# A residual attention block with a three-cycle coupling network: the later weights' loads move behind the first transposes of x, and every engine's list of steps is in a new order

## What is computed

```python
def reference(x, ctx, ...):
    x = x + xattn(layernorm(x), ctx, ctx, Wq, bq, Wk, bk, Wv, bv, Wo, bo, phase)
    return x + ffn(layernorm(x), cn_w1, ..., gc_b3, adaptive_range)

def xattn(q, k, v, ...):
    qh, kh, vh = heads(q @ Wq.T + bq), heads(k @ Wk.T + bk), heads(v @ Wv.T + bv)
    qh, kh = phase_sync(qh, phase), phase_sync(kh, phase)
    attn = softmax(einsum('bhqd,bhkd->bhqk', qh, kh) / sqrt(32))
    return merge(einsum('bhqk,bhkd->bhqd', attn, vh)) @ Wo.T + bo

def ffn(x, ...):
    gf = global_net(x.mean(axis=1))            # gelu, gelu, sigmoid
    out = x
    for _ in range(3):
        tf = coupling_net(out)                 # w1, w2, w3 with gelu, w4 with sigmoid
        coupling = 0.1 + adaptive_range * (0.7 * gf + 0.3 * tf - 0.5) * 2.0
        out = out + coupling * twist(out)      # swaps quarters of the columns
    return out
```

## Time and profile before

| | us |
|---|---|
| median of 3 runs | 1389.52 |
| lowest, highest | 1389.43, 1393.32 |
| the profiled execution | 1389.49 |
| its span, first to last instruction | 1387.7 |
| PE busy (of the span) | 1248.0 (90%) |
| DVE busy | 1071.4 (77%) |
| ACT busy | 1059.0 (76%) |
| POOL busy | 624.0 (45%) |

### The profile page before, as it was taken

The page is one execution under the profiler, slowest core; times in us unless marked ns, Lnnn a source line. Parts: engine busy times, 40 slices in busy tenths (PEclk is TensorE's granted clock), DMA queues, the critical chain, the costliest instruction groups (busy, mean ns, idle before and its releaser), DMA issues.

```text
span 1387.7 us, 27846 instructions
## 1 busy us (share of the span) xinstructions
PE 1248.0 (90%) x10392; PEld 863.4 (62%) x10392; DVE 1071.4 (77%) x2125; ACT 1059.0 (76%) x1912; POOL 624.0 (45%) x491
## 2 busy tenths in 40 slices
PE   7776889989999899999999899999999899999984
PEld 5332556657666676658666666657666666657763
DVE  3897449986799769996799769995799759984465
...
DMA packets 319065, 116.54 MB, mean 84 GB/s; under 512 B 301777, under 2 KB 303569, under 8 KB 316882
## 3 DMA queue, kind: packets, MB, share of 16 engines
...
...
## 4 chain that ended last, share of the span: by engine, by line
PE 44%; DVE 18%; ACT 15%; issue 9%; SPq 6%; DMA 6%; POOL 2%; ACTq 0%; DVEq 0%; POOLq 0%
PE ps L369 15%; PE ps L384 9%; PE ps L269 7%; PE ps L318 6%; SPq L3070 3%; PE ps L396 3%; ACT spent L776 2%; DVE xr L1829 2%; DMA x2T<-xr 2%; SPq L3024 2%; PE ps L287 2%; PE ps L404 2%; ACT xr L764 2%; ACT z L848 2%; DVE pr L1871 2%
## 5 line engine op out<-in xcount | busy, mean ns | idle before, releaser
L2869 POOL TENSOR_TENSOR h<-z,h 128x512 f16<-128x512 f32 x192 | 251.3, 1314 | 355.8 <-DVE h L1919 355.8
L369 PE MATMUL ps<-x2T,W 128*128 128x256 f16 x3072 | 350.5, 274 | 5.6 <-ACT Y L835 2.2
L369 PEld LDWEIGHTS ps<-x2T,W 128*128 128x128 f16 x3072 | 297.7, 98 | 54.7 <-issue 9.6
L384 PE MATMUL ps<-h,W 128*128 128x256 f16 x2304 | 275.1, 275 | 12.6 <-POOL h L2869 11.3
L384 PEld LDWEIGHTS ps<-h,W 128*128 128x128 f16 x2304 | 223.5, 99 | 62.7 <-issue 26.5
L2862 POOL TENSOR_TENSOR prob<-prob,rc 128x512 f32<-128x512 f32 x128 | 147.5, 1174 | 140.0 <-DVE rc L1865 140.0
L269 PE MATMUL ps<-xoT,WQ 128*128 128x512 f16 x768 | 176.2, 383 | 16.3 <-DMA xoT<-xr 10.4
L318 PE MATMUL ps<-WO,xoT 128*128 128x512 f16 x768 | 179.6, 384 | 7.2 <-DVE xoT L1876 7.2
L1829 DVE TENSOR_TENSOR xr<-ps,xr 128x512 f16<-128x512 f32 x128 | 87.9, 687 | 82.9 <-ACT xr L764 81.6
L269 PEld LDWEIGHTS ps<-xoT,WQ 128*128 128x128 f16 x768 | 73.6, 98 | 104.6 <-DMA xoT<-xr 11.5
L318 PEld LDWEIGHTS ps<-WO,xoT 128*128 128x128 f16 x768 | 75.0, 99 | 97.7 <-DVE xoT L1876 8.1
...
## 6 DMA issues: line engine op xcount, KB each, us to landing
xin<-x SPq DMA_DIRECT2D x16, 1024.0 KB, 5.2
...
pT<-pr SPq DMA_TRANSPOSE x128, 3.2
wq_s<-wq SPq DMA_DIRECT2D x1, 1024.0 KB, 5.7
wk_s<-wk SPq DMA_DIRECT2D x1, 1024.0 KB, 10.1
```

The lines of the kernel that those rows point to most:

```text
L369: mm = e.matmul(ps[:, BANK_F + L, at * LBLK:(at + 1) * LBLK], w, v, start=(n == 0), stop=(n == 3 * C - 1))
L384: mm = e.matmul(ps[:, BANK_F + L, m * LBLK:(m + 1) * LBLK], w, v, start=(c + m + a == 0), stop=(c == C - 1 and m == C2 - 1 and a == 2))
L2869: e.tensor_tensor(h1[:, L, LO, pair(n)], z[:, L, pair(n)], h1[:, L, HI, pair(n)], ALU.subtract).then_inc(lg[L]["lo1"], 1)
```

## The change

SP gets a new step, `load_late(n)`. The seventeen loads that stood in a row ahead of the first `x_turn` (the output weight and bias, the last rows of weights, three scalars, w1, w2, g1, w3, g2 and five bias columns) are dealt out to five calls of it, behind the first turns of x:

```diff
             load_x(1)
-            load("wo", wo_s[:], by_chunk(woT))
-            load("bo", bo_s[:], row(bo).partition_broadcast(P))
...
-            load("cols", gb2_col[:], gb2)
-            x_turn(0, 0, 0, 0); x_turn(0, 0, 0, 1); x_turn(0, 0, 0, 3); x_turn(0, 0, 0, 2)
-            kv_load(0)
-            kv_store(0, 1)
-            x_turn(0, 0, 1, 0); x_turn(0, 0, 1, 1); x_turn(0, 0, 1, 2); x_turn(0, 0, 1, 3)
+            x_turn(0, 0, 0, 0); x_turn(0, 0, 0, 1); x_turn(0, 0, 0, 2); x_turn(0, 0, 0, 3)
+            load_late(0, 1); load_late(0, 3); load_late(0, 0); load_late(0, 2)
+            x_turn(0, 0, 1, 0)
+            kv_store(0, 1)
+            kv_load(0)
+            x_turn(0, 0, 1, 1)
+            load_late(0, 4)
+            x_turn(0, 0, 1, 3); x_turn(0, 0, 1, 2)
```

All engines' lists are in a new order beyond that. On PE `q(0,0,3)` stands one `vmul` earlier, the first `y` of the network are (0,0,1,0), (0,0,1,1), (0,0,0,0), and in batch 1 `y(0,0,1,3)` goes ahead of `s(1,0)` and an `l2` between `s(1,0)` and `s(1,1)`. On DVE `zero_v` is spread between the first `xl`, `bias_out` is earlier, and the output bias and the last rows of weights come behind `k_lo`. On SP in batch 0:

```diff
-            p_turn(0, 4, 0); p_turn(0, 4, 1); p_turn(0, 5, 0); p_turn(0, 5, 1); p_turn(0, 6, 0); p_turn(0, 6, 1)
-            load_next(0, 0)
-            p_turn(0, 7, 0); p_turn(0, 7, 1)
+            p_turn(0, 4, 0); p_turn(0, 4, 1); p_turn(0, 5, 0); p_turn(0, 5, 1)
+            kv_store(0, 5)
+            p_turn(0, 6, 0)
+            load_next(0, 0)
+            p_turn(0, 7, 0); p_turn(0, 6, 1); p_turn(0, 7, 1)
```

More of the change, by code:

```diff
@@ L1120, in scalar_program @@
             gg(1, 0)
+            t_out(0, 0, 1, 0)
+            act1(1, 0, 0, 0, 0)
+            t_out(0, 0, 1, 1)
+            act1(1, 0, 1, 0, 0)
             act3(0, 1, 1, 2)
-            t_out(0, 0, 1, 0); t_out(0, 0, 1, 1)
             yc(1, 0, 0, 1)
-            act1(1, 0, 0, 0, 0); act1(1, 0, 0, 0, 1); act1(1, 0, 1, 0, 0)
+            act1(1, 0, 0, 0, 1)
+            xn1(2, 0, 0)
             gg(1, 1)
-            t_out(0, 1, 0, 0)
+            xh(2, 0, 0, 0)
             u_(0, 1, 1, 2)
+            cc(0, 1, 1, 2)
@@ L1142, in scalar_program @@
             xh(2, 0, 0, 3)
[L1143 to L1144 removed]
+            yc(1, 0, 0, 3)
+            act1(1, 0, 0, 0, 3)
+            t_out(0, 1, 0, 1)
+            act1(1, 1, 0, 0, 0)
             yc(1, 1, 0, 1)
[L1146 to L1149 removed]
+            act2(1, 0, 0, 0, 0); act2(1, 0, 0, 0, 1)
             xn1(2, 1, 0)
             xh(2, 0, 1, 0)
+            t_out(0, 1, 1, 0)
@@ L1280, in scalar_program @@
                 gg(p, 0)
-                t_out(o, 0, 1, 0); t_out(o, 0, 1, 1)
+                act1(p, 0, 0, 0, 0); act1(p, 0, 1, 0, 0)
+                t_out(o, 0, 1, 0)
+                act3(o, 1, 1, 2)
+                t_out(o, 0, 1, 1)
                 yc(p, 0, 0, 1)
-                act1(p, 0, 0, 0, 0)
-                act3(o, 1, 1, 2)
-                act1(p, 0, 0, 0, 1); act1(p, 0, 1, 0, 0)
+                act1(p, 0, 0, 0, 1)
+                xn1(b, 0, 0)
                 gg(p, 1)
+                xh(b, 0, 0, 0)
@@ L2288, in vector_program @@
-            stats(2, 0, 1, 3)
-            aggr(2, 0, 1, 2); aggr(2, 0, 1, 3)
-            var(2, 0, 1)
-            hi1(1, 0, 0, 0, 1)
-            coef(0, 1, 1)
-            nm(2, 0, 1)
-            ql(2, 0, 0)
+            aggr(2, 0, 0, 1)
+            gv(1, 1)
+            aggr(2, 0, 0, 2); aggr(2, 0, 0, 3)
+            outs(0, 0, 1, 0)
+            var(2, 0, 0)
+            outs(0, 0, 1, 1)
+            hi1(1, 0, 0, 0, 0)
+            nm(2, 0, 0)
+            xl(2, 0, 0, 0)
+            gv(1, 2)
@@ L2295, in vector_program @@
+            hi1(1, 0, 1, 0, 0)
+            xl(2, 0, 0, 1)
+            stats(2, 0, 1, 0); stats(2, 0, 1, 1); stats(2, 0, 1, 2)
+            xl(2, 0, 0, 2)
+            stats(2, 0, 1, 3)
+            coef(0, 1, 0)
+            xl(2, 0, 0, 3)
+            hi1(1, 0, 0, 0, 1)
+            aggr(2, 0, 1, 0); aggr(2, 0, 1, 1); aggr(2, 0, 1, 2); aggr(2, 0, 1, 3)
+            var(2, 0, 1)
+            alph(1)
+            nm(2, 0, 1)
+            coef(0, 1, 1)
+            outs(0, 1, 0, 0)
             xl(2, 0, 1, 0)
-            ql(2, 0, 1)
@@ L2665, in vector_program @@
             pl(7, 1)
-            sub(7, 3, 0)
+            mxs(7, 3, 0)
             ql(7, 1, 0)
@@ L3109, in p_turn, with load_late @@
                 e.dma_start_transpose(pT[:, part, :, cols(j)], pr[:, n % 2, part]).then_inc(p_turned[n % 2], 16)
+            @first
+            def load_late(n):
+                if n == 0:
+                    load("wo", wo_s[:], by_chunk(woT))
+                elif n == 1:
+                    load("bo", bo_s[:], row(bo).partition_broadcast(P))
+                    load("last", last_s[:, 0:1], cw4)
+                    load("last", last_s[:, 1:2], gw3)
+                    for i, a in enumerate((arange, cb4, gb3)):
+                        load("scal", scal_s[:, i:i + 1], row(a).partition_broadcast(P))
+                elif n == 2:
+                    load("w1", w1_s[:], by_chunk(cw1))
+                elif n == 3:
+                    load("w2", w2_s[:], by_chunk(cw2))
+                    load("g1", gw1_s[:], by_chunk(gw1))
+                    load("w3", W3[:], by_chunk(cw3))
+                    load("g2", gw2_s[:], by_chunk(gw2))
+                else:
+                    load("cols", b1_col[:], cb1)
+                    load("cols", b2_col[:], cb2)
+                    load("cols", b3_col[:], cb3)
+                    load("cols", gb1_col[:], gb1)
+                    load("cols", gb2_col[:], gb2)
             ctx_view = ctxT.rearrange("(c p) b n -> p c b n", p=P)
```

1668 lines of the change are left out of this document (808 added, 860 removed).

## The result

The changed kernel takes **1367.2 us** (1367.1 to 1367.8), the kernel before in the same comparison 1391.0 (1389.4 to 1393.3): 23.8 us or 1.7% less, ratio 0.983 with an interval of 0.981 to 0.985. The forecast was 1375.5, 14.0 less, in a range of 1365 to 1387. The sign and the range held; 10 us of the gain had not been foreseen, and the time lies outside the 1370 to 1384 that the forecast's own case, A, had. The profiled execution has a span of 1366.0 against 1387.7 us, so the two traces have to account for 21.7.

A forecast was written before the change was run, and what follows sets the result against it. PE, busy 1248.0 of 1387.7 us, bounds the kernel, with a hole at the start behind late weight loads and DVE pacing 75 to 109 us. -10.5 - 1.8 - 0.5 - 1.2 = -14.0 gives 1375.5 us, range 1365 to 1387.

The forecast's parts named there:

- A: Whole program, the forecast itself: the start's gain arrives and the loop is neutral, 1370 to 1384 us; chance 0.66.
- The first turns: Start: turns of x without late loads ahead land in 3.2 us; first `q` at 34.2 instead of 43.46 us.
- The rival within A: Start: first turns take 5.1 us because six loads are not through; start gives -8, time 1378 us; no separate chance.
- PE, ACT, DVE behind them: Start, up to DVE's full stretch: first `s` 12.8 us earlier, second 10.5, the stretch moves whole: -10.5 us.
- The late loads' cover: Start: late weights issued from about 29 us make ACT wait a few us at worst; at most 1 us shows.
- Case C: Start: late weights hold ACT and DVE, so the gain is given back: 1385.3 to 1391 us; chance 0.13.
- Batch 0's last turn: End of batch 0: load of x issued earlier, so the softmax's last turn isn't 6.18 us: -1.8, between 0 and -3.0.
- Batch 1: Batch 1: `y(0,0,1,3)` ahead of `s(1,0)` against two more ACT table loads: -0.5 us, between -1.7 and +2.6.
- The loop: Six loop passes in new order: PE nearly full, -0.2 us a pass, -1.2 in all, between -12 and +18.
- case B: Loop: reordered `l2`, `l3`, `l4` remove 1.5 to 2 us of waits a pass: 1364 to 1367 us; chance 0.12.
- D: Loop: load of x ahead of the softmax's last turns delays them 3.0 us a pass: 1394.7 us; chance 0.09.
- The end: End of the program: last stores and factors move within their own waits: 0, within 2 us.

The follow-up runs named there:

- The experiment with the loads alone: Kernel before with only SP's late loads moved behind the four first turns of x, all other lists old: 1396.1 us, ratio 1.003.
- the seam: Where new lists change to old ones: at the first query product of batch 1, 1378.9 us; at that of batch 2, 1376.7 us.
- a run in the new loop: Changed kernel with DVE's `coef` ahead of `gv` again in five passes: 1366.8 us.
- two of the runs above: Kernel before with only the late loads moved, 1396.1 us; a later variant of the changed kernel with the first tile's scores ahead of a `vmul`, 1366.4 us.

## Why the prediction was right, and where it was not

**The first turns.** Said: ready at 21.5, landing in 3.2, first `q` at 34.2 with 2.75 us and a clock of 1.00. Measured: issue at 20.95, median landing 3.1 us, `q` at 33.20 with 2.75 us, clock 1.00. The rival within A, 5.1 us a turn, did not come; the six loads were through by then.

**PE, ACT, DVE behind them.** `k_hi(0)` at 26.94 (said 27.8), `k_lo` at 31.52 (32.0), first `s` at 61.38 (62.4), second at 66.27 (68.1), just ahead of the 67 to 69 that would show it. The later `q` that was at 84.94 is at 72.41, 12.5 us earlier where 10.5 was taken: the first `s` was 13.8 instead of 12.8 earlier, and 1.5 us were lost between the tiles instead of the 2.3 that I had put down for weights there. DVE's stretch moved nearly as a whole: the last `s` is still 11.5 earlier (111.69 and 100.16 us).

**The late loads' cover.** Twelve of them left from 29.21 to 36.4 us, at 0.4 to 0.6 us each for most, the rate of an empty queue, and `wo` took 8.3 us to land instead of 14.4. It landed at 42.6, 2.3 us ahead of `w_hi(0)`. Case C needed the full queue's rate and didn't occur. The experiment with the loads alone shows what the cover is worth: without ACT's new order the same loads cost 17 us of waiting and the whole gain.

**Batch 0's last turn.** Said -1.8, from 6.18 to 3.2. The chain of waits that ended last, before, ahead of the turn of 127.23 us and behind it:

```profile
125.92 1.26 SPq L3109
...
133.50 1.23 PE ps L303 x24
```

and in the changed kernel, 112 to 124 us:

```profile
115.38 3.18 SPq L3111
...
118.62 3.19 DMA pT<-pr
...
121.90 0.89 PE ps L303 x24
```

The turn lands in 3.19 us as said, but it leaves only 8.6 us earlier, where the last `s` had been 11.5 earlier. 1.9 of those 2.9 us are the turn's issue on SP, 3.18 instead of 1.26 us behind the load of x. So the `pv` is 11.6 us earlier, no more than the start had given already: the load's price had gone from the landing into the issue. `wo(4)` behind it is 12.4 earlier (140.34 and 127.96). Start and tail together were said to be 12.3 and measured 12.0, with two errors that cancel, which is luck: -10.5 should have been about -11.5, and -1.8 about -0.5.

**Batch 1.** Said -0.5 between -1.7 and +2.6, measured -1.9 by trace against the kernel before, -2.2 at the seam by times and -3.5 by ratios: beyond the lower end. The term left out that the old order gives 1.8 us of an early start back.

**The loop.** This is the term that was mis-sized: -1.2, with ends -12 and +18, measured -9.3 over six passes, or -7.8 with the end, to which some of PE's work has moved. The step that failed is "PE's work is the same and it is nearly full, so I take -0.2 a pass". The 4.5 us of waits for ACT at lines 396 and 404 in a pass were the right place to look, and 1.6 of them went per pass (18.1 to 11.5 us in four), which is case B's size. Nor was PE's busy time the same: it is some 0.6 us a pass less for the same products. But the reason given for B was wrong: the `l2` and `l4` in that stretch cost 6.0 us and don't gain. D's mechanism was real and 0.3 to 0.6 us a pass instead of 3.0. With both taken off, the rest of the new loop order (ACT's whole list, the `y` and `l2` between the `s`, `l4` right behind `pv`) must be worth some 17 us (an estimate, 7.8 + 6.0 + 2.8), if the parts add up, which was not tested.

The range held because it had been drawn down from A's 1370 into B's 1364 to 1367: the measured 1367.2 lies between the two. And by the sign that I had set, a pass more than 1 us off its old length, the loop's order counts as well as the start: four of its six passes are 1.1 to 3.1 us shorter.

**What stays open.** Which of those moves brings it. `gv` is excluded by a run in the new loop. The others hang together across engines, and a list changed on one engine alone makes another wait, as two of the runs above show; they were not tried one by one. Some 1.3 us of it, in one pass, can be the clock's short dip.

**The end.** Said 0 within 2. The 1.5 us given back behind batch 7's mark in this one trace are within that, and seven other traces with the same lists don't show them.
